# Causal attention with a gated feed-forward block on one Trainium2 core: single transposes between the 512-column score passes, the accumulator's bank as a third transpose bank in the middle slots, and two small tiles typed float32r

## The reference

```python
q, k, v = einsum('bsx,xMnd->Mbnsd', x, qkv)
a = einsum('bnsd,bntd->bnst', q, k) * D ** -0.5
cum = cumsum(rpe_bias[:, :S], axis=-1)
rel = arange(S)[:, None] - arange(S)[None, :]
bias = where(rel >= 0, cum[:, clip(rel, 0)], -30000.0)
mix = einsum('bnst,bntd->bnsd', softmax(a + bias), v)
x1 = layernorm(x + einsum('bnsd,ndx->bsx', mix, out_w))
xr = mu_r * x1 + (1 - mu_r) * shifted(x1)      # shifted: the previous token
xk = mu_k * x1 + (1 - mu_k) * shifted(x1)
y = sigmoid(xr @ W_r) * (square(relu(xk @ W_k)) @ W_v)
out = layernorm(x1 + y)
```

## Time and profile before

| | |
|---|---|
| median of 3 runs | 1118.04 us (1117.57 to 1122.45) |
| the profiled execution | 1117.19 us, span 1115.4 us |
| PE busy | 1061.8 us, 95% of the span |
| ACT, DVE, POOL busy | 70%, 67%, 9% |
| granted PE clock, mean | 0.984 of full |

### The profile page before, as it was taken

One profiled execution on the slowest core, in us unless ns is written; L12 is line 12 of the kernel. 1 busy time (PEld: TensorE's weight loads), 2 busy tenths in 40 slices (PEclk: granted clock), 3 DMA queues, 4 the chain that ended last, 5 costly groups with the idle time before them and its releaser, 6 DMA issues.

```text
span 1115.4 us, 21793 instructions
## 1 busy us (share of the span) xinstructions
PE 1061.8 (95%) x6975; PEld 754.3 (68%) x6975; DVE 748.1 (67%) x1977; ACT 778.0 (70%) x1998; POOL 97.3 (9%) x103
## 2 busy tenths in 40 slices
PE   5899999999999999999999999999999999999995
PEld 3665666766666776676777676677676677666774
DVE  2665566665657677666777776767766767776667
ACT  3766677776767787776777777677676777777743
POOL 1000000000000111010011100011100011100100
PEclk8999999999999999999999999999999999999997
DMA  7755666666667767667676766676756676765810
GB/s 183 177 148 151 181 166 172 167 148 163 163 154 174 181 158 181 159 160 186 159 182 157 178 155 159 168 178 171 181 137 163 168 172 161 183 157 152 243 62 21
DMA packets 116223, 180.73 MB, mean 162 GB/s; under 512 B 13680, under 2 KB 72960, under 8 KB 116112
## 3 DMA queue, kind: packets, MB, share of 16 engines
q1 hardware_dynamic: 112992, 176.85, 63.3%
q10 hardware_dynamic: 3120, 2.49, 0.9%
HBM read 58.41 MB, written 20.22 MB: 70 GB/s over the span
## 4 chain that ended last, share of the span: by engine, by line
PE 66%; DMA 11%; SPq 8%; ACT 6%; issue 4%; DVE 3%; POOL 2%; DVEq 0%; ACTq 0%
PE ps_o L1106 21%; PE ps_rows L1065 16%; PE ps_t L1082 9%; PE ps_m L1040 8%; DMA stacks<-k_lo 7%; SPq L316 5%; PE ps_m L1122 4%; PE ps_m L1045 3%; ACT prob L566 3%; PE ps_o L1082 2%; ACT pt L584 2%; POOL mix_sb L494 2%; DVE pt L779 1%; SPq L386 1%; PE ps_rows L1161 1%
## 5 line engine op out<-in xcount | busy, mean ns | idle before, releaser
L761 DVE CUSTOM_DVE_ANT_0 prob<-ps_rows,table 128x128 f32<-128x128 f32 (+7 forms) x512 | 379.8, 750 | 104.5 <-PE ps_rows L1065 84.8
L566 ACT ACTIVATE prob<-prob,low 128x128 f32<-128x128 f32 (+7 forms) x512 | 394.4, 772 | 44.0 <-DVE low L761 39.7
L1065 PE MATMUL ps_rows<-stacks 128*128 128x512 f32 (+3 forms) x1536 | 396.8, 370 | 15.3 <-DMA stacks<-k_lo 8.0
L1082 PE MATMUL ps_t<-ident_r,prob_r 128*128 128x128 f32 x1984 | 284.5, 263 | 6.9 <-ACT pt L584 3.1
L1082 PEld LDWEIGHTS ps_t<-ident_r,prob_r 128*128 128x128 f32 x1984 | 213.2, 142 | 88.3 <-issue 71.8
L1065 PEld LDWEIGHTS ps_rows<-stacks 128*128 128x128 f32 x1536 | 246.8, 191 | 36.0 <-DMA stacks<-k_lo 10.9
L1106 PE MATMUL ps_o<-pt,v_pair 128*64 128x512 f32 (+3 forms) x1536 | 268.9, 492 | 0.0
L779 DVE COPY pt<-ps_t 128x512 f32<-128x512 f32 (+3 forms) x288 | 165.0, 582 | 147.5 <-PE ps_t L1082 147.5
L1106 PEld LDWEIGHTS ps_o<-pt,v_pair 128*64 128x64 f32 x1536 | 101.7, 136 | 176.4 <-issue 164.1
L584 ACT ACTIVATE pt<-ps_t 128x512 f32<-128x512 f32 (+3 forms) x384 | 175.2, 456 | 30.8 <-PE ps_t L1082 29.4
L494 POOL TENSOR_TENSOR mix_sb<-mix_sb,inv_all 128x512 f32<-128x512 f32 x64 | 82.2, 1285 | 923.8 <-ACT mix_sb L608 923.8
(11 more groups left out here) (127 smaller groups left out, 675.1 us busy)
## 6 DMA issues: line engine op xcount, KB each, us to landing
stacks<-k_hi SPq DMA_DIRECT2D x124, 256.0 KB, 4.5
stacks<-k_lo SPq DMA_DIRECT2D x124, 256.0 KB, 5.1
inv_all<-inverse_sums SPq DMA_DIRECT2D x128, 128.0 KB, 3.4
stacks<-q_hi SPq DMA_DIRECT2D x62, 256.0 KB, 3.5
stacks<-q_lo SPq DMA_DIRECT2D x62, 256.0 KB, 4.4
mix_transposed<-mix_sb SPq DMA_DIRECT2D x62, 256.0 KB, 3.8
table<-bias_by_distance SPq DMA_DIRECT2D x64, 192.0 KB, 3.8
mix_tile<-mix_transposed SPq DMA_DIRECT2D x24, 448.0 KB, 3.9
```

Source lines behind the costliest of these rows:

```text
L566: nc.scalar.activation(row, row, ACT.Exp, bias=low[:, r:r + 1], scale=-1.0, accum_out=total[:, r:r + 1]).then_inc(s_exp, 1)
L761: nc.vector.tensor_tensor_reduce(prob[:, r % PSLOTS, 0:width], ps_rows[:, score_at(r):score_at(r) + width], table[n % 2][:, h, 0:width][:, ...
L1065: ins = nc.tensor.matmul(ps_rows[:, at + c0:at + c1], q_st(h, n)[:, P * i:P * i + P], k_st(h, n, low_part)[:, c0:c1], start=(low_part == 0 ...
L1082: ins = nc.tensor.transpose(t_bank[TBANK[k]][:, P * b:P * b + P].bitcast(F32R), prob_r[:, r % PSLOTS, at:at + P], ident_r[:, :])
```

## The change

Four edits.

1. The passes of a score row are issued one by one. In slots 3, 6, 7, 10, 11 and 15 (`AMONG`) one transpose of the slot's own row is issued behind each pass of 512 columns (in slot 6 behind the passes of 384 columns too), as long as blocks are left; the rest of the row's transposes stay at the end of the slot. By slot that moves 2, 3, 4, 2, 4 and 2 transposes, 17 in a step. In slots 3, 7, 10 and 15 the moved ones now stand ahead of the projection, in slot 11 ahead of the mix.
2. `TBANK` becomes `[0, 1] * 4 + [0, 2, 1, 0, 2, 1, 0, 1] * 2`. So `ps_o` takes banks 9 and 12 between the copy of the far mix and the near mix, and banks 17 and 20 after the near mix (before: 16, 19 and 22). Banks 9 and 17 wait for the copy of the mix result, bank 12 for the evacuation of bank 9. The near mix waits, among others, for the evacuation of bank 12.
3. On ACT, slot 11 now copies out bank 14, then takes the exponential of row 15, then copies the near mix; before it was the exponential, the mix copy, the bank.
4. `inv` and `x1` share memory with tiles typed float32r, and their transposes are done in that type against `ident_r`.

The diff, cut to its core (for the second and third edit a line or two):

```diff
-TBANK = [k % 2 for k in range(16)] + [2, 0, 1, 2, 0, 1, 2, 1]
+TBANK = [0, 1] * 4 + [0, 2, 1, 0, 2, 1, 0, 1] + [0, 2, 1, 0, 2, 1, 0, 1]
+BEHIND_MIX = (9, 17)
...
+AMONG = (3, 6, 7, 10, 11, 15)
...
+            def passes(r):
+                at, width = score_at(r), P * (ROWS[r][1] + 1)
+                cut = min(BANK - at % BANK, width)
+                return [(c0, max(c1, c0 + SHORTEST), low_part) for c0, c1 in ((0, cut), (cut, width)) if c0 < c1
+                        for low_part in range(2)]
...
-                    if TBANK[k] == 2 and 2 not in TBANK[:k]:
-                        pe.wait_ge(s_raw, 2 * n + 2)
+                    if k in BEHIND_MIX:
+                        pe.wait_ge(s_raw, 2 * n + 1 + BEHIND_MIX.index(k))
...
-                        ins = nc.tensor.transpose(t_bank[TBANK[k]][0:2 * GROUP, 3 * P:],
-                                                  inv[:, 2 * GROUP * g:2 * GROUP * (g + 1)], ident[:, :])
+                        ins = nc.tensor.transpose(bank[0:2 * GROUP, 3 * P:],
+                                                  inv_r[:, 2 * GROUP * g:2 * GROUP * (g + 1)], ident_r[:, :])
...
-                        ins = nc.tensor.transpose(t_bank[TBANK[k]][:, P:2 * P], x1[:, :], ident[:, :])
+                        ins = nc.tensor.transpose(bank[:, P:2 * P], x1_r[:, :], ident_r[:, :])
...
-                    for row in rows_ahead(n, more, slot):
-                        score(*row)
+                    blocks = ROWS[slot][1] + 1
+                    moved = 0
+                    for m, row in rows_ahead(n, more, slot):
+                        for which in range(len(passes(row))):
+                            score(m, row, which)
+                            c0, c1, _ = passes(row)[which]
+                            share = min(1, blocks - moved) if slot in AMONG and c1 - c0 >= BANK - P * (slot == 6) else 0
+                            for block in range(moved, moved + share):
+                                transpose(n, slot, block, tile_too)
+                            moved += share
...
-                    transpose(n, slot, tile_too)
+                    for block in range(moved, blocks):
+                        transpose(n, slot, block, tile_too)
```

More of the change, by code:

```diff
@@ L124, in build @@
         prob = sb("prob", [P, PSLOTS, SEQ])
+        with nc.sbuf_tensor("inv_r", [P, NROWS], F32R) as inv_r:
+            pass
+        inv = sb("inv", [P, NROWS])
+        with nc.sbuf_tensor("x1_r", [P, C], F32R) as x1_r:
+            pass
+        x1 = sb("x1", [P, C])
         ident = sb("ident", [P, P])
@@ L636, in step @@
                         copy_mix(n - 1, 1)
-                    if slot == MIX_NEAR:
-                        for row in rows_ahead(n, more, slot):
-                            exps(*row)
-                        copy_mix(n, 0)
                     for k in range(NBANKS):
@@ L645, in step @@
                         tile_step(n, RK_PROJ)
-                    if slot != MIX_NEAR:
-                        for row in rows_ahead(n, more, slot):
-                            exps(*row)
+                    for row in rows_ahead(n, more, slot):
+                        exps(*row)
+                    if slot == MIX_NEAR:
+                        copy_mix(n, 0)
             drive(step)
@@ new lines, in score @@
+            def score(n, r, which):
+                h, i = ROWS[r]
+                if which == 0:
+                    if n == 0 and i == 0:
+                        pe.wait_ge(s_first[h], 96)
+                    elif i % GROUP == 0:
+                        pe.wait_ge(s_stack[h], 96 * n + 96)
+                    pe.wait_ge(s_biased, NROWS * n + r + 3 - rows_since(r))
+                c0, c1, low_part = passes(r)[which]
+                at = score_at(r)
+                ins = nc.tensor.matmul(ps_rows[:, at + c0:at + c1], q_st(h, n)[:, P * i:P * i + P],
+                                       k_st(h, n, low_part)[:, c0:c1], start=(low_part == 0), stop=(low_part == 1))
+                if which == len(passes(r)) - 1:
+                    ins.then_inc(s_score, 1)
@@ L1077, in transpose @@
+            def transpose(n, r, block, tile_too):
+                k = next(k for k in range(NBANKS) if BANKS[k][0] == r and BANKS[k][1] == block // 4 * 4)
+                _, b0, nb = BANKS[k]
+                bank = t_bank[TBANK[k]].bitcast(F32R)
+                if block == 0:
+                    pe.wait_ge(s_exp, NROWS * n + r + 1)
+                if block == b0:
+                    if k in BEHIND_MIX:
+                        pe.wait_ge(s_raw, 2 * n + 1 + BEHIND_MIX.index(k))
                     else:
@@ L1140, in _ @@
             for r in range(LEAD):
-                score(0, r)
+                for which in range(len(passes(r))):
+                    score(0, r, which)
             pe.wait_ge(s_in_w, 64)
```

32 lines of the change are left out of this document (5 added, 27 removed).

## The result

The kernel with the change takes 1131.77 us (median of seven runs, 1129.75 to 1135.35), the kernel before in the same session 1118.18 us. The ratio is 1.0112, with a 95% interval of 1.0089 to 1.0134: slower by 1.1%, near the forecast (1129). The span of the profiled execution is 1129.0 us, against 1115.4 before, so 13.6 us are to be found.

The account below looks back on a forecast made before the run. PE, busy 95% of the span, was taken as the bound. Steps 9 to 30 10.8, steps 0 to 8 6.4, last step 0.4: 17.6 us, less 1.3 (types) and 5 (DMA), +11.3: 1129 us, own range 1123 to 1136, overall 1110 to 1137.

Parts of the forecast that it names:

- The lone transpose: A single transpose between two passes costs 0.12 us against 0.084 in a run: surcharge 0.035 per added run, bounds 0.027 and 0.07.
- Rival A: The lone transpose hides, the pass behind it taking 0.23 us: about -6 us, 1112; chance 0.24.
- C: Rival, dearer boundaries: a surcharge of 0.07 us for each added run of transposes, 1142 us; chance 0.12.
- Slot 8: The fifth transpose's 0.29 us wait for bank 9 goes, since bank 9 in ps_o waits for the far mix's copy.
- DVE's chain: Slots 6 to 10: row 10 and bias 12 0.36 us later; PE waits, row 14 starts 0.14 later, 0.36 in early steps.
- Rival B: DVE's chain shortens, so row 14 starts at 500.33, 0.12 us before: +2 us, 1120; chance 0.18.
- Early steps: Steps 0 to 8, with no slack before row 14: 0.71 us each, 6.4 us in all.
- The third bank at the end of the step: Bank 17 needs the near mix's copy, which starts as before; bank 14's evacuation fits in ACT's wait for row 15: nothing.
- The types: float32r transposes of inv (279 ns) and x1 (275) fall to 263: at most 1.3 us less, taken in full.
- DMA: Waits for stacks, 18 times, 10.9 us: k copies do not move while PE comes later; 0 to 6 us back, 5 taken.
- Slot 0: Forecast to stay as it was, difference 0; slot 15 was charged 0.07 us per step.
- The range: 1123 to 1136 us for the forecast itself: surcharge 0.027 gives 4 less, DMA waits giving nothing 5 more.

Follow-up runs that it names:

- middle_bank: Kernel before plus the float32r types and the third bank in the middle slots only; old ACT order, no moved transposes: 1117.05 us, 0.9988.
- middle_slot_6: Kernel with the third bank in the middle slots only and the types, plus only slot 6's moved transposes: 1121.48 us, 1.0014 of the kernel before.
- banks_old_act: Changed kernel without any moved transposes and with ACT's slot 11 order as before; new banks and types stay: 1116.89 us, 0.9994 of the kernel before.
- banks_only: Changed kernel with AMONG empty, so no moved transposes; new banks, new ACT order and types stay: 1151.51 us, 1.0284 of the kernel before.

## Why the forecast was right, and where it was not

- **The lone transpose** costs what was worked out: 0.11, a surcharge of 0.03 for each boundary (forecast 0.035). Slots 3, 10, 11 and 12 to 15 sum to 0.32 where 0.35 was forecast, and slots 3 and 10 alone gave 0.14 for four. Rival A (it hides) and C (0.07) are out. That the load of the next pass is what shows is the forecast's reading; no run isolates it. The Trainium skill (TensorE: Matmul & The Clock Gate, section "Architectural detail: the array is 16× 32×32, not 1× 128×128") lets PE pull LDWEIGHTS ahead of in-flight matmuls; the trace agrees for one load (a pass behind a pass takes 0.23, its load is not seen), not for two in a row (a pass behind a lone transpose takes 0.28).
- **Slot 8** lost its wait, as forecast; in middle_bank that is worth 0.33 (forecast 0.29).
- **DVE's chain turned the gain into a wait.** It moved by 0.29 (forecast 0.36), row 14 stands 0.06 to 0.07 behind bias 12 in every step from 0 to 30, and PE waits ahead of it. Some 0.04 of the difference lie in the point it is counted from: with the types slot 6's first pass itself starts that much later behind the transpose of `inv`, and between middle_bank and middle_slot_6, which both have them, the chain moves by 0.34. Slots 4 to 9 give +0.14, as forecast. Rival B (DVE gives way) is out: the chain keeps its length to 0.01 us. What I had not seen is a second cause for the same delay: I let `k_hi` move with ACT's exponential, but it also waits for slot 7's projection, which four moved transposes hold up. The sum was right since the two lie side by side.
- **Early steps**: steps 0 to 8 are 5.0 longer, with 1.3 of `stacks` waits given back, so 6.3 where 6.4 was forecast before any DMA. The sum agrees, its parts do not: slots 4 to 9 took 3.8 more (forecast 3.2), slots 0 to 3 2.7 more (0.6), and slots 10 to 15, without the DMA, 0.1 less (2.5 more). I have not traced the last two to a cause; that they cancel is luck.
- **The third bank at the end of the step** cost nothing, as forecast, but for a reason that the forecast gave only half: bank 16 follows bank 14 in `ps_t0`, and in banks_old_act, where ACT takes bank 14 behind the mix copy, it waits 0.36; the new order spares that wait. Bank 17 is not held up by the new order only because slot 11's transposes have moved; without them it waits for the mix copy, as banks_only shows. What the old order costs with the moves in place was not run.
- **The types**: the term of -1.3 is wrong, the starts show no gain. It took a difference of record lengths for a difference of starts.
- **DMA**: 5 forecast to come back; the list of waits gave 6.8 back, 5.5 of them in steps 9 to 30. The reason given holds: SP issues the copies of k 5.16 behind slot 6's first pass (508.61 - 503.45), before 5.26, so they are no later while PE is.

```profile
508.61 1.24 SPq L322 DMA_DIRECT2D stacks<-k_hi  x2
```

- **Slot 0** is the step that failed: slot 15 was charged 0.07 for its boundaries and nothing for what stands behind it (the sum holds "if nothing else binds"). The wait for the V projection's copy adds 0.17 x 22 = 3.7 us, a fourth of the result. The types (1.3 not won) and the ends of the run (1.0 where 0.4 was forecast) add to it. DMA waits (1.8 more given back), the other slots of the table (0.6), other single waits (0.8) and the early steps (0.1) take 3.3 of these 5.6 back; that leaves the 2.3 us between 13.6 and the forecast's 11.3.
- **The range** of 1123 to 1136 is wider than its own terms, which give 4 below and 5 above; the result does not hang on that.

That the two whole-kernel numbers agree is therefore partly luck: five of six lines of the table agree, but the sixth, 3.7 us, is larger than the whole distance between forecast and result.
